# Adding the residual and the shared expert on GpSimd instead of the Vector engine in the last combination, and running 79 routed tiles instead of 80

## The reference, cut to what matters

```
logits = x2 @ gate_w.T                       # 16 experts
top_w, top_i = top_k(softmax(logits), 4)     # 4 experts per token, weights normalised to sum 1
gu  = x2 @ w1[e].T ; act = silu(g) * u       # per expert, 176 wide
down = act @ w2[e].T                         # back to 256
routed = sum over the 4 experts of weight * down
shared = (silu(sg) * su) @ sh_down_w.T       # one shared expert for every token
x_out = x + tanh(g_ffn) * (hid + routed + shared)
```

## Time and profile before

| | |
|---|---|
| median of the three timed runs | 993.75 us (993.18 to 994.84) |
| the profiled execution | 991.21 us, its span 989.3 us |
| PE busy over the span | 865.2 us, 87% |
| DVE / ACT / POOL busy over the span | 79% / 67% / 52% |
| routed tiles | start of the scatters 811.6 us, last scatter 956.3 us |
| combination | first read issued 958.8 us, last sum ends 986.6 us |
| output landed | 988.8 us (last transfer issued at 986.6, landed 2.2 us later) |

### The profile page before, as it was taken

One profiled execution on the slowest core, in us unless ns is written; L12 is line 12 of the kernel. 1 busy time (PEld: TensorE's weight loads), 2 busy tenths in 40 slices (PEclk: granted clock), 3 DMA queues, 4 the chain that ended last, 5 costly groups with the idle time before them and its releaser, 6 DMA issues. The chain is left out here.

```text
span 989.3 us, 23819 instructions
## 1 busy us (share of the span) xinstructions
PE 865.2 (87%) x8200; PEld 616.3 (62%) x8200; DVE 784.0 (79%) x1925; ACT 662.3 (67%) x1611; POOL 513.7 (52%) x608
## 2 busy tenths in 40 slices
PE   3466689999999998999999899998999589999970
PEld 1233356777777676676767677676765357777750
DVE  5788978878788888989998776778867777777738
ACT  3678868888887777778788676666653136666640
POOL 5688873556456364777745264210542615555550
PEclk8576569999999999999999999999999889999996
DMA  5322410101000010122000123014131534444439
GB/s 180 97 78 73 144 62 23 30 23 49 20 13 27 23 51 8 56 83 71 25 15 10 64 91 123 35 27 140 55 129 43 192 107 150 153 155 143 142 131 358
DMA packets 47827, 84.08 MB, mean 85 GB/s; under 512 B 6448, under 2 KB 36528, under 8 KB 47664
## 3 DMA queue, kind: packets, MB, share of 16 engines
q1 hardware_dynamic: 39792, 61.60, 19.7%
q0 software_dynamic: 6912, 19.93, 5.7%
q10 hardware_dynamic: 1008, 1.03, 0.3%
HBM read 52.92 MB, written 31.98 MB: 86 GB/s over the span
## 5 line engine op out<-in xcount | busy, mean ns | idle before, releaser
L665 PE MATMUL ps<-whi,ar 128*128 128x256 f16 (+1 forms) x800 | 226.6, 283 | 18.8 <-DVE ar L1765 9.5
L667 PE MATMUL ps<-whi,ar 128*128 128x256 f16 (+1 forms) x800 | 226.3, 283 | 0.0
L666 PE MATMUL ps<-wlo,ar 128*128 128x256 f16 (+1 forms) x800 | 226.2, 283 | 0.0
L1544 POOL TENSOR_TENSOR ar<-ar,sm 128x512 f32<-128x512 f32 x64 | 69.8, 1091 | 157.8 <-DVE sm L1831 157.8
L1459 POOL TENSOR_TENSOR sm<-sm,mhalf 128x1 f32<-128x1 f32 (+2 forms) x72 | 125.4, 1741 | 6.0
L665 PE MATMUL ps<-ar 128*128 128x128 f16 (+1 forms) x768 | 117.7, 207 | 8.9 <-DVE ar L1715 4.4
L1595 POOL DMA_INDIRECT y<-ar,idx x80 | 76.9, 962 | 90.8 <-ACT ar L1429 76.4
L666 PE MATMUL ps<-ar 128*128 128x128 f16 (+1 forms) x768 | 117.5, 206 | 0.0
L667 PE MATMUL ps<-ar 128*128 128x128 f16 (+1 forms) x768 | 117.5, 206 | 0.0
L665 PE MATMUL ps<-ar,whi 128*128 128x512 f16 x292 | 112.3, 385 | 0.1
L667 PE MATMUL ps<-ar,wlo 128*128 128x512 f16 x292 | 112.0, 383 | 0.0
(11 more groups left out here) (236 smaller groups left out, 2277.6 us busy)
## 6 DMA issues: line engine op xcount, KB each, us to landing
ar<-xg SPq DMA_DIRECT2D x80, 144.0 KB
ar<-in_wall SPq DMA_DIRECT2D x16, 512.0 KB, 3.7
stg<-in_wall SPq DMA_DIRECT2D x32, 188.0 KB, 2.5
ar<-in_wall SPq DMA_DIRECT2D x8, 608.0 KB, 4.5
whi<-y SPq DMA_DIRECT2D x4, 1024.0 KB, 8.8
wlo<-y SPq DMA_DIRECT2D x4, 1024.0 KB, 17.5
xg<-in_pad SPq DMA_DIRECT2D x1, 2304.0 KB
xg<-x1d SPq DMA_DIRECT2D x4, 512.0 KB, 4.2
```

The costliest lines, as they stand in the source:

```text
L665: mm(o, l_hi, r_hi, start=start, stop=False, skip_group_check=True)
L666: mm(o, l_hi, r_lo, start=False, stop=False, skip_group_check=True)
L667: return mm(o, l_lo, r_hi, start=False, stop=stop, skip_group_check=True)
L1544: TT(pr, pr, eq4.unsqueeze(2).broadcast_to([P, GB, S]), ALU.mult).then_inc(sem("p_n"), 1)
```

## The change

The diff makes two edits. First, `add_z` leaves DVE's program and becomes eight instructions at the end of POOL's program, behind the last `s_lo`; it waits on the same two semaphores. DVE keeps only the two steps of `mix`. Second, the second tile of the last pair (tile number 79, counting from 0) is left out by SP, PE and POOL: `tiles(39)` is 1. ACT and DVE still work on both halves of the pair's buffers. The semaphore counts that others wait for are lowered to match.

```diff
+LIVE = NB * TOPK + NE - 1

+        def tiles(u):
+            return min(2, LIVE - 2 * u)
...
@@ SP
-                for i, r in enumerate((both & 511, both >> 9)):
+                for i, r in enumerate((both & 511, both >> 9)[:tiles(u)]):
                     r = (r * P).with_bounds(min_val=0, max_val=SLOTS - P)
                     sp.dma_start(xinw[v][:, i, :], xg[bass.ds(r, P), :]).then_inc(sem(f"xin{v}"), 16)
...
-                sp.wait_ge(sem(f"y_put{b}"), 32 * (PAIRS // 2))
+                sp.wait_ge(sem(f"y_put{b}"), 16 * sum(tiles(u) for u in range(b, PAIRS, 2)))
@@ PE: turn_tile, gate_up, turn_m and down_tile, each
-                for i in range(2):
+                for i in range(tiles(u)):
@@ PE, in the loop over the pairs; DVE the same in select
-                    turn_tile(u + 2, (u + 2) % 4, 32 * ((u + 2) // 4 + 1))
+                    turn_tile(u + 2, (u + 2) % 4, 32 * ((u + 2) // 4) + 16 * tiles(u + 2))
@@ POOL
+            def add_z(m):
+                pool.wait_ge(sem("y_sum"), 2 * m + 2)
+                pool.wait_ge(sem("fin"), m // 2 + 1)
+                TT(ob[m], ob[m], zfin[m // 2][:, m % 2 * 512:m % 2 * 512 + 512], ALU.add).then_inc(sem("mixed"), 1)
...
-                for i in range(2):
+                for i in range(tiles(u)):
                     nc.gpsimd.indirect_dma_start(
...
             s_lo(SHL, 2)
+            for m in range(NB // 2):
+                add_z(m)
@@ DVE
-            def add_z(m):
-                dve.wait_ge(sem("y_sum"), 2 * m + 2)
-                dve.wait_ge(sem("fin"), m // 2 + 1)
-                TT(ob[m], ob[m], zfin[m // 2][:, m % 2 * 512:m % 2 * 512 + 512], ALU.add).then_inc(sem("mixed"), 1)
...
                 mix(m)
                 if m == 1:
                     s_add(SHL)
-                add_z(m)
```

More of the change, by code:

```diff
@@ L2168, in _ @@
                     take(u + 2, u % 2)
-                    select(u + 2, (u + 2) % 4, 32 * ((u + 2) // 4 + 1))
+                    select(u + 2, (u + 2) % 4, 32 * ((u + 2) // 4) + 16 * tiles(u + 2))
                 lo_tile(u, u % 2)
```

## The result

The changed kernel is slower. Ten timed runs of it have a median of 999.55 us, ten of the kernel before 994.26; the ratio is 1.0047 with a 95% interval of 1.003 to 1.0063, so about +4.7 us (3.0 to 6.3; the medians are 5.3 apart). The forecast was 993.05 us, that is -0.7 against the 993.75 it started from, with a range from 991.4 to 995.2. The profiled execution took 996.47 us (span 994.6) against 991.21 (span 989.3).

The account below looks back on a forecast made before the run. It took DVE to bound the combination, the reads nearly tied. 1.93 us gained until m = 2, less 0.65 for slower m and 0.5 for the hand-over, with 0.08 for a landing, gave -0.7: 993.05 us, range 991.4 to 995.2.

Parts of the forecast that it names:

- the end of the chain: Behind the last add_z on POOL, ending at 985.91 against 986.61, only the output transfer of 2.2 us follows.
- The shared access: In the combination, POOL's and DVE's sums exclude each other; add_z adds 1.02 us behind DVE, DVE's second step 0.54.
- The pace: Time per m of the combination in a steady state: 2.70 us, against 2.587 before.
- hand-over: At the end of the combination, passing from DVE's last second step to POOL's last add_z loses 0.5 us.
- The stricter reading: In the combination, each sum holds the shared port for its whole duration, so an m costs 3.06 us; chance 0.10.
- The tile: Part one: leaving out tile 79 issues the combination's first read 1.72 us earlier, at 957.1; bounds 1.27 and 1.9.
- The landings: Arrivals of the combination's eight reads, 2.53 us a read, all moved 1.72 us earlier.
- near tie: In the combination, DVE's 2.587 us an m nearly equals the reads' 2.53, so a faster DVE alone soon waits for data.
- Rival 1: In the combination, DVE and POOL don't hold each other up: -1.75 us, 992.0 us; chance 0.27 together with Rival 4.
- rival 2: In the combination, whole durations add on the shared port: 3.06 us an m, +1.0, 994.8 us; chance 0.10.
- rival 3: Reads don't start 1.72 us earlier, as ACT or the scatter's landing takes it back: 994.3 us; chance 0.08.
- Rival 4: POOL's share is smaller, landings decide from m = 3 on: 992.0 to 992.5 us; chance 0.27 together with Rival 1.

Follow-up runs that it names:

- e3: Kernel before, with one late wait for the eighth 'mixed' added at the end of POOL's program; ratio 1.0059 (1.0038 to 1.0081) against the kernel before.
- e4: Kernel before, with an explicit drain on POOL behind the last s_lo, then the late wait of e3; ratio 1.0001 (0.9983 to 1.0019) against the kernel before.
- e9: e4 with one POOL sum of 512 columns behind the late wait; closing drain 1.26 us including that sum, which leaves 0.1; its time isn't used.
- e10: e4 with one indirect transfer of 128 rows on POOL behind the late wait; closing drain at most 0.14 us; its time isn't used.
- e12: e10 with 16 indirect transfers behind the late wait instead of one; closing drain 1.36 us; its time isn't used.
- e1: Changed kernel with add_z back on DVE, so only tile 79 left out; ratio 0.9985 (0.9965 to 1.0005) against the kernel before, read to output 30.6 us.
- e5: Changed kernel with add_z left out on every engine, 79 tiles; ratio 0.9953 (0.9937 to 0.997) against the kernel before, read to output 28.5 us.

## Why the prediction was wrong

**The step that failed** is the end of the chain. The prediction says of POOL that "the eight instructions queue behind nothing; what stands behind them is the output transfer", and then "The output transfer keeps its 2.2 us". Behind POOL's last instruction stands the closing drain as well, and it is longer: 6.6 us against 2.2. It wasn't in the sum, nor in any rival. The row was in the trace of before, from 964.3 for 8.4 us, under a line that none of the views by cost list, because a drain isn't counted as busy. e3 and e4 show its price alone: +0.59% where it stands at the end and nothing where it is hidden. Of the 6.0 us between the forecast and the profile (-0.7 against +5.3) it is 4.2; the combination is 0.7 to 0.8, the first read 0.4, and 0.7 arose before the first scatter.

**The shared access.** Right in kind: the sums excluded each other, DVE's second step took 1.63 us (forecast "some 1.5"), POOL's 2.18 (forecast "some 2.1"), and those of m = 1 and 7 ran free. The pace was mis-sized: 2.81 instead of 2.70, because an `add_z` adds 1.12 behind DVE's sum where I took the 1.02 of `s_lo`. Alone it took 1.26, not 1.15. The prediction calls `s_lo` a sum with two 32-bit operands, which it isn't: it reads a 32-bit and a 16-bit one (`me_p` and `me_hl`, line 1527) and writes 16 bits. Which of these differences makes `add_z` slower no run shows. From the first `mix` to the end of the last sum I had 985.91 - 962.48 = 23.4 us, measured 987.80 - 963.53 = 24.3. That is the 0.8 us of the miss. The prediction's split of its -0.7 (1.93 gained, 0.65 lost in five slower m, 0.5 in the hand-over, 0.08 for a landing) doesn't come out of its own timeline: from the start of m = 2 to that of m = 7 it has 981.9 - 969.08 = 12.82 us against 12.93 before, and from there to the end 4.01 against 2.67. The total is right. The stricter reading of the Trainium skill, "SBUF — State Buffer", section "Who interferes with whom", by which whole durations add, had given in the prediction 3.06 us an m, and would give 1.22 + 1.26 + 0.69 = 3.17 with the sum's measured time; the trace has 2.81, so whole recorded durations don't add here. That the two exclude each other, as the section says, the trace confirms.

**The tile.** 1.72 us forecast for the first read. The one profile of the changed kernel gives 1.3, the means of all profiles 1.5 to 1.8. Right in size, though six of the kernels with 80 tiles, whose programs are the same up to the first read (before, e3, e4, e9, e10, e12), differ by 1.5 us among themselves in this stretch. DVE's first sum profits less, as forecast (30.6 against 30.3 in e1).

**The landings.** Forecast as the near tie behind DVE; e5 shows it, at 2.56 us a read. In the changed kernel they decided nothing, since POOL was later.

**Rival 1** (no mutual cost) is refuted by the second steps of 1.63 us, rival 2 by the pace, rival 3 by the 145.9 us. Rival 4 didn't come up either: the landings never set the pace.

## What to carry to other kernels

Before work goes to the end of an engine's program, read what the engine still does when its program is over. Here GpSimd's close took 0.08 us for each of the 79 or 80 indirect transfers of its last stage, and it belongs ahead of the last long stage or under it. A second engine helped here only beside an instruction that read PSUM: that one sum cost 0.1 us at its tail, while two engines whose sums excluded each other needed 0.2 us an m more than one engine doing all. And of an engine at 91% in a stage (20.41 of 22.40 us), ask for the next bound first: of 5.5 us of work only 2.1 could be had.

## What was not expected of the hardware

- GpSimd's drain grew with the indirect transfers issued since the drain before: 0.14 us for 1, 1.36 for 16, 5.3 for 64, 6.59 for 80, and 0.04 with none. Without a drain between, the 64 of the routing added nothing to the 80 of the tiles (6.60 in e3), which stays open. The transfers had all landed long before, in e3 by some 28 us (the first read, which waits for them, was issued at 960.3, the drain began at 988.2), so it isn't a wait for data.
- A GpSimd sum of 512 columns took 1.26 us with two 32-bit operands and a 32-bit result (`add_z`), and 1.15 with one 32-bit and one 16-bit operand and a 16-bit result (`s_lo`).
- A semaphore wait late on an engine that has nothing more to do cost as much as the whole change, within the intervals: e3 is 0.59% slower than before (0.38 to 0.81), the changed kernel 0.47% (0.30 to 0.63).
